# A graph attention layer: q and k as a 257th column of each half of the projection, row scales transposed later

## The reference

```python
h = jnp.maximum(_layernorm(x, axis=-1), 0.0)
q = jnp.einsum('c,bcn->bn', wq, h)
k = jnp.einsum('c,bcn->bn', wk, h)
scores = q[:, None, :] + k[:, :, None]
scores = jnp.where(scores > 0, scores, 0.01 * scores)
att = jax.nn.softmax(scores, axis=-1)
agg = jnp.einsum('bcn,bmn->bcm', h, att)
out = x + jax.nn.relu(jnp.einsum('oc,bcm->bom', wm, agg) + bm[None, :, None])
```

## Time and profile before

| | us |
|---|---|
| median of 3 runs (2089.21 to 2089.91) | 2089.28 |
| the profiled execution, its own time | 2090.47 |
| its span, first to last instruction | 2088.7 |
| PE busy | 2051.5 (98%) |
| DVE busy | 1674.8 (80%) |
| ACT busy | 1221.5 (58%) |
| POOL busy | 379.6 (18%) |
| 3 groups of unit matmuls (L385 to L387), 2048 each | 776 each |
| 3 groups of v tile matmuls (L362 to L364), 1024 each | 389 each |

### The profile page before, as it was taken

How to read it: one execution, slowest core, us unless ns; L and a number is a source line. 1 busy time by engine, 2 the same in 40 slices (tenths; PEclk the granted TensorE clock), 3 DMA queues, 4 the chain that set the end, 5 groups by cost and what they waited for, 6 DMA issues and landing times.

```text
span 2088.7 us, 33534 instructions
## 1 busy us (share of the span) xinstructions
PE 2051.5 (98%) x10448; PEld 950.3 (45%) x10448; DVE 1674.8 (80%) x3661; ACT 1221.5 (58%) x1871; POOL 379.6 (18%) x273
## 2 busy tenths in 40 slices
PE   5899999999999999999999999999999999999999
PEld 2344444444444444444444444444444444444444
DVE  7978878778887788887788877888877888778853
ACT  5556656556655566565566555665655665556634
POOL 1012211112111122111121111221111211112212
PEclk9999999999999999999999999999999999999999
DMA  5244433344324444333433234442334432343332
GB/s 195 64 155 142 148 99 123 138 160 141 133 84 136 151 141 146 104 118 137 161 141 133 84 136 151 141 146 105 117 137 161 141 131 86 136 152 141 106 101 76
DMA packets 126395, 271.46 MB, mean 130 GB/s; under 512 B 22624, under 2 KB 23136, under 8 KB 122208
## 3 DMA queue, kind: packets, MB, share of 16 engines
q1 hardware_dynamic: 123904, 269.01, 37.1%
q10 hardware_dynamic: 2400, 1.58, 0.3%
HBM read 202.91 MB, written 67.63 MB: 130 GB/s over the span
## 4 chain that ended last, share of the span: by engine, by line
PE 95%; DVE 3%; DMA 1%; POOL 0%; issue 0%; ACT 0%; POOLq 0%; SPq 0%; DVEq 0%
PE mix L385 21%; PE mix L387 21%; PE mix L386 21%; PE mix L362 10%; PE mix L363 10%; PE mix L364 10%; PE small L325 2%; DVE den_out L728 1%; PE small L334 1%; DMA xs<-in_x_dram 0%; DVE p_ring L749 0%; DVE p_lo L756 0%; DVE v_lo L761 0%; POOL wm_nat L893 0%; DMA den_row<-den_rows 0%
## 5 line engine op out<-in xcount | busy, mean ns | idle before, releaser
L385 PE MATMUL mix<-p_hi,v_hi 128*128 128x512 f16 x2048 | 776.3, 379 | 5.9 <-DVE p_lo L756 5.4
L386 PE MATMUL mix<-p_lo,v_hi 128*128 128x512 f16 x2048 | 776.2, 379 | 0.0
L387 PE MATMUL mix<-p_hi,v_lo 128*128 128x512 f16 x2048 | 776.2, 379 | 0.0
L911 POOL TENSOR_TENSOR res<-res,y 128x512 f32<-128x512 f32 x256 | 370.5, 1447 | 1688.2 <-ACT y L512 1688.2
L749 DVE SCALAR_TENSOR_TENSOR p_ring<-ab_row,cols,p_ring 128x512 f32<-128x512 f32 x512 | 377.1, 748 | 129.7 <-ACT p_ring L491 129.7
L491 ACT ACTIVATE p_ring<-ab_row,cols 128x512 f32<-128x512 f32 x512 | 349.5, 691 | 192.4 <-DMA ab_row<-ab_rows 132.3
L503 ACT ACTIVATE v_hi<-mix 128x512 f16<-128x512 f32 x256 | 152.7, 597 | 444.1 <-PE mix L364 443.5
L728 DVE SCALAR_TENSOR_TENSOR den_out<-den_row,cols 128x512 f32<-128x512 f32 x512 | 393.4, 806 | 1.0 <-DMA den_row<-den_rows 1.0
L362 PE MATMUL mix<-wmT_hi,h_hi 128*128 128x512 f16 x1024 | 389.1, 380 | 0.0
L364 PE MATMUL mix<-wmT_hi,h_lo 128*128 128x512 f16 x1024 | 388.8, 380 | 0.0
L363 PE MATMUL mix<-wmT_lo,h_hi 128*128 128x512 f16 x1024 | 388.8, 380 | 0.0
(11 more groups left out here) (71 smaller groups left out, 838.9 us busy)
## 6 DMA issues: line engine op xcount, KB each, us to landing
res<-in_x_dram SPq DMA_DIRECT2D x256, 256.0 KB, 3.2
out_dram<-res SPq DMA_DIRECT2D x256, 256.0 KB, 2.1
xs<-in_x_dram SPq DMA_DIRECT2D x124, 512.0 KB, 6.5
den_row<-den_rows SPq DMA_DIRECT2D x32, 1024.0 KB, 4.6
ab_row<-ab_rows SPq DMA_DIRECT2D x64, 512.0 KB, 5.0
res<-in_x_dram SPq DMA_DIRECT2D x4, 512.0 KB, 5.0
wm_nat<-in_adj_dram ACTq DMA_DIRECT2D x1, 1024.0 KB, 12.2
den_rows<-cols SPq DMA_DIRECT2D x32, 8.0 KB, 1.6
```

The costliest lines, as they stand in the source:

```text
L385: pe.matmul(ps[:, :], v_hi[:, b[1], nt, chans], p_hi[:, hf, nt, :], start=(nt == 0), stop=False)
L386: pe.matmul(ps[:, :], v_hi[:, b[1], nt, chans], p_lo[:, hf, nt, :], start=False, stop=False)
L387: mm = pe.matmul(ps[:, :], v_lo[:, b[1], nt, chans], p_hi[:, hf, nt, :], start=False, stop=(nt == NT - 1))
L911: pool.tensor_tensor(res[:, k, :], res[:, k, :], y[:, k % 2, :], ALU.add).then_inc(s_add, 1)
```

## The change

The weights of q and k become a 257th column in each half of the transposed projection weights. A v tile is then 24 matmuls of 257 columns, into a pair of banks, where it was 12 matmuls of 512 into one; with two pairs instead of four banks, tile nt waits for `v_lower` of tile nt-2, and the first two tiles for relu 4 and 5, and for relu 6 and 7. `project_qk` and `select_qk` go away, except that the first batch has a short projection of its own (96 matmuls of two columns). ACT copies the two extra columns out ahead of each `v_upper`. As q and k are complete only with the last tile, `q_head`, `q_tail`, `exponentials` and the trip of the denominators' rows move into the following period; denominators stand behind half 1 as a block. `spread_qmax` moves into unit 0, `transpose_ab` in unit 5 from node tile 2 to node tile 5. ACT's `h_upper`, `h_full` and relu 1 and 2 move behind half 1; relu 6 goes behind step 3 of half 0, relu 7 and `v_upper` 0 behind step 5; `v_lower` 0 goes behind DVE's step 5. At the start POOL scales two of four weight tiles and the q and k weights, DVE scales the other two.

```diff
-        wmT_hi = sb("wmT_hi", [P, CT, O], F16)
-        wmT_lo = sb("wmT_lo", [P, CT, O], F16)
+        wmT_hi = sb("wmT_hi", [P, CT, 2, OH + 1], F16)
+        wmT_lo = sb("wmT_lo", [P, CT, 2, OH + 1], F16)
...
+        pair = [ctx.enter_context(nc.psum_tensor(f"pair{i}", [P, 2, 512], F32)) for i in range(2)]
+        mix = [pair[i // 2][:, i % 2, :] for i in range(MIX)]
...
             def period(b, one, two, three):
+                if one:
+                    write_den_rows(nxt(b))
+                    load_den_rows(nxt(b))
...
-                if two:
-                    write_den_rows(nxt(b, 2))
-                    load_den_rows(nxt(b, 2))
...
+            def project_first_qk():
+
+                pe.wait_ge(s_wqk, 2)
+                pe.wait_ge(s_hlo, CT)
+                for nt in range(NT):
+                    for ct in range(CT):
+                        nodes = slice(nt * P, (nt + 1) * P)
+                        hi, lo = h_hi[:, 0, ct, nodes], h_lo[:, 0, ct, nodes]
+                        w_hi, w_lo = wmT_hi[:, ct, :, OH], wmT_lo[:, ct, :, OH]
+                        pe.matmul(qk_ps[:, nt, :], hi, w_hi, start=(ct == 0), stop=False)
+                        pe.matmul(qk_ps[:, nt, :], hi, w_lo, start=False, stop=False)
+                        mm = pe.matmul(qk_ps[:, nt, :], lo, w_hi, start=False, stop=(ct == CT - 1))
...
             def v_tile(b, nt):
 
-                if nt < MIX and at(b, second):
-                    pe.wait_ge(s_vlo[nt % 2], (nt + MIX) // 2 + 1)
-                elif nt < MIX:
-                    wait(pe, s_y[nt % 2], cnt(b, U // 2, (nt + MIX) // 2 + 1 - U))
+
+                if nt == 0:
+                    pe.wait_ge(s_hlo, cnt(b, CT, CT))
+                if nt < 2 and at(b, second):
+                    pe.wait_ge(s_vlo[nt], NT // 2)
+                elif nt < 2:
+                    for i in range(2):
+                        wait(pe, s_y[i], cnt(b, U // 2, nt + 3 - U))
                 else:
-                    pe.wait_ge(s_vlo[nt % 2], cnt(b, NT // 2, (nt - MIX) // 2 + 1))
-                ps, nodes = mix[nt % MIX], slice(nt * P, (nt + 1) * P)
+                    pe.wait_ge(s_vlo[nt % 2], cnt(b, NT // 2, nt // 2))
+                ps, nodes = pair[nt % 2], slice(nt * P, (nt + 1) * P)
                 for ct in range(CT):
                     if nt == 0 and at(b, first):
-                        pe.wait_ge(s_wl, ct + 1)
+                        pe.wait_ge(s_wl, max(2, ct + 1))
                     hi, lo = h_hi[:, b[1], ct, nodes], h_lo[:, b[1], ct, nodes]
-                    pe.matmul(ps[:, :], hi, wmT_hi[:, ct, :], start=(ct == 0), stop=False)
-                    pe.matmul(ps[:, :], hi, wmT_lo[:, ct, :], start=False, stop=False)
-                    mm = pe.matmul(ps[:, :], lo, wmT_hi[:, ct, :], start=False, stop=(ct == CT - 1))
+                    for half in range(2):
+                        pe.matmul(ps[:, half, 0:OH + 1], hi, wmT_hi[:, ct, half, :],
+                                  start=(ct == 0), stop=False)
+                    for half in range(2):
+                        pe.matmul(ps[:, half, 0:OH + 1], hi, wmT_lo[:, ct, half, :], start=False, stop=False)
+                    for half in range(2):
+                        mm = pe.matmul(ps[:, half, 0:OH + 1], lo, wmT_hi[:, ct, half, :],
+                                       start=False, stop=(ct == CT - 1))
...
                 elif one:
-                    pe.wait_ge(s_vlo[k % 2], cnt(nxt(b), NT // 2, (k + MIX) // 2 + 1))
+                    pe.wait_ge(s_vlo[k // 2], cnt(nxt(b), NT // 2, NT // 2))
                 else:
                     pe.wait_ge(s_y[k % 2], cnt(b, U // 2, (k + MIX) // 2 + 1 - U // 2))
                 ps, chans = mix[k % MIX], slice(ot * P, (ot + 1) * P)
                 for nt in range(NT):
-                    if one and k == MIX + 1 and nt == 2:
+                    if one and k == MIX + 1 and nt == 5:
                         transpose_ab(nxt(b))
+                    if one and (k, nt) == ((1, 2) if at(b, first) else (0, 3)):
+                        spread_qmax(nxt(b))
...
             def v_upper(b, nt):
+
                 act.wait_ge(s_v, cnt(b, NT, nt + 1))
-                act.activation(v_hi[:, b[1], nt, :], mix[nt % MIX][:, :], ACT.Copy,
+                ps = pair[nt % 2]
+                if not at(b, first):
+                    act.activation(qk4[:, nt, :], ps[:, :, OH], ACT.Copy)
+                act.activation(v_hi[:, b[1], nt, :].rearrange("p (h o) -> p h o", h=2), ps[:, :, 0:OH], ACT.Copy,
                                scale=1.0 / H_SCALE).then_inc(s_vhi, 1)
...
                     p_upper(b, NT + nt)
                     if nt < NT - 2:
                         leak(b, NT + nt + 2)
-                    if two and nt in (0, 3, 7):
-                        h_upper(h, (0, 3, 7).index(nt))
-                    if two and nt in (1, 5):
-                        h_full(h, nt // 4)
-                    if nt in (2, 4, 6):
-                        relu(b, nt // 2 - 1)
+                    if one and nt == 1:
+                        exponentials(nxt(b))
+                    if nt == 5:
+                        relu(b, 0)
                 if two:
+                    h_upper(h, 0)
+                    h_full(h, 0)
+                relu(b, 1)
+                if two:
+                    h_upper(h, 1)
+                    h_full(h, 1)
+                relu(b, 2)
+                if two:
+                    h_upper(h, 2)
                     h_upper(h, 3)
                 relu(b, 3)
                 if two:
@@ -543,17 +535,19 @@
                             leak(n, nt + 2)
                         if nt == 0:
                             relu(b, 5)
-                        if nt == 4:
+                        if nt == 3:
                             relu(b, 6)
+                        if nt == 5:
+                            relu(b, 7)
+                            if two:
+                                v_upper(h, 0)
                 else:
                     relu(b, 5)
                     relu(b, 6)
-                relu(b, 7)
+                    relu(b, 7)
                 if two:
-                    for nt in range(NT):
+                    for nt in range(1, NT):
                         v_upper(h, nt)
-                        if nt == 4:
-                            exponentials(h)
...
             def q_head(b):
-                dve.wait_ge(s_qk, cnt(b, 2, 2))
-                for i in range(2):
-                    ins = dve.tensor_copy(qk[:, i, :].rearrange("p (g c) -> p c g", c=2), qk_ps[:, :, :, i])
-                    if i == 0:
-                        q_link(b, 2, ins)
+
+                if at(b, first):
+                    dve.wait_ge(s_qk, 1)
+                    dve.tensor_copy(qk4[:, :, :], qk_ps).then_inc(s_qf, 1)
+                    dve.wait_ge(s_qf, 1)
+                    dve.wait_ge(s_un, 1)
+                else:
+                    dve.wait_ge(s_vhi, cnt(b, NT, NT))
+                q_link(b, 1, dve.tensor_scalar(qk[:, 0, :], qk4[:, :, 0], unscale_q[:, 0:1], None, ALU.mult))
+                dve.tensor_scalar(qk[:, 1, :], qk4[:, :, 1], unscale_q[:, 1:2], None, ALU.mult).then_inc(s_qc, 1)
...
-            def half_0(b):
+                dve.scalar_tensor_tensor(out=v_lo[:, b[1], nt, :].rearrange("p (h o) -> p h o", h=2),
+                                         in0=pair[nt % 2][:, :, 0:OH], scalar=1.0 / H_SCALE,
+                                         in1=v_hi[:, b[1], nt, :].rearrange("p (h o) -> p h o", h=2),
+                                         op0=ALU.mult, op1=ALU.subtract).then_inc(s_vlo[nt % 2], 1)
+
+            def half_0(b, two):
                 weight(b, 0)
                 for nt in range(NT):
                     if nt < NT - 1:
                         weight(b, nt + 1)
                     p_lower(b, nt)
+                    if two and nt == 5:
+                        v_lower(nxt(b), 0)
 
             def early(b, one, two):
                 h = nxt(b, 2)
+                if one:
+                    q_head(nxt(b))
                 weight(b, NT)
                 for nt in range(NT):
                     if nt < NT - 1:
                         weight(b, NT + nt + 1)
-                    if one:
+                    p_lower(b, NT + nt)
+                    if one and nt == 0:
+                        q_tail(nxt(b))
+                if one:
+                    for nt in range(NT):
                         denominator(nxt(b), nt)
-                    p_lower(b, NT + nt)
-                if one:
                     row_scales(nxt(b))
                 if two:
                     h_lower(h, 0)
@@ -792,65 +781,60 @@
             def late(b, one, two, three):
                 h = nxt(b, 2)
                 if one:
-                    half_0(nxt(b))
+                    half_0(nxt(b), two)
                 if two:
-                    q_rows(h)
-                    for nt in range(NT):
```

(65 more changed lines are left out.)

114 lines of the change are left out of this document (31 added, 83 removed).

## The result

The changed kernel takes 2127.27 us (median of 4, 2125.04 to 2128.97) where the kernel before takes 2089.24 (2088.99 to 2089.91) on the same chip: a ratio of 1.0181, 95% interval 1.0163 to 1.0198. It is slower, by 38 us, where 24.5 were forecast.

The account below looks back on a forecast made before the run. PE's own list was taken to set the time. 30 periods by +0.6 (18), start +4.5 and end +2 make 24.5 over the profiled 2090.47: 2115, or 2114 us against the median; range 2060 to 2140.

Parts of the forecast that it names:

- the forecast case: PE waits for relu 7 in each projection, a period of 64.4 us for 63.83; 2105 to 2125 us, chance 63%.
- Sign and mechanism: Slower, since PE stands 1.6 us in v tile 1 of each projection, waiting for ACT's relu 7.
- the late transpose moves relu 7 itself: Transpose at 29.23 us after unit 0, formerly 27.19, delays copy and relu 7; at node tile 2 almost no wait.
- row scales to 25.2: On DVE, half 1 of p and then 16 half denominators leave the row scales ready 25.2 us after unit 0.
- the loss to POOL: Some 0.9 us lost to POOL during the 16 half denominators on DVE, which take 0.67 each.
- PE's list: PE's work per period falls from 63.83 to 62.68 us, with 257-column matmuls at 0.1094 each.
- the small wait: Before unit 0 PE waits for v_lower 6, behind the normaliser on DVE: 0.16 us a period.
- Weight loads under 257 columns: In the projection, loads of 0.10 us hide under matmuls of 0.109; rival that they don't fully, 2142 to 2167, 12%.
- The small waits: Around unit 0: 0.16 us for v_lower 6, and nothing or at most 0.2 for the spread's input.
- Start: First batch and its delays: +4.5 us, between 0 and +19.
- The end: In the last batches, without a projection, half 0 comes 2 us later: +2 us.
- The sum: Whole kernel: 18 us from 30 periods, 4.5 at the start, 2 at the end, together 24.5 us slower.

## Why the prediction was right, and where not

The kernel got slower, as forecast. 2127 lies in the range of 2060 to 2140 and 2 us above the 2105 to 2125 that the forecast case was given.

- **Sign and mechanism: right.** PE stands before the 25th v matmul with ACT's y as releaser, 1.56 us in the period read above (1.6 forecast), with the copy at 29.70 (29.56), the leak at 35.58 (35.54), relu 7 from 45.06 to 45.88 (45.0 to 45.8). Moving relu 7 alone takes the loss away.
- **Why relu 7 is late: wrong step.** "... the late transpose moves relu 7 itself; with the transpose left at node tile 2 the wait would be near nothing." It was not: 2126.75. The failed step is "row scales to 25.2", where 27.4 was measured. The half rows cost 0.673 as forecast, but the loss to POOL is 3.0 us, not the 0.9 of the earlier trace rows and its neighbours: as a block behind half 1, denominators meet three of POOL's adds (at 557.54, 560.40 and 564.27), inside half 1 they met one a period (93 of 512 half rows are long in the changed kernel, 30 before). With h_lower 0 and 1 behind the row scales DVE was busy until 29.70, just when the late transpose would have held it. The dates agreed by luck, because two causes fell on the same one. Where the loss is taken away, the sentence is true: with POOL's adds narrow and the transpose at node tile 2 the wait is 3.5 us in all, 2081.25. The Trainium skill (GPSIMD Engine Reference, "Specifications") lists GpSimd's memory interfaces as shared with VectorE, with contention for DVE instructions that have two SBUF inputs; a denominator has two (both rows of `den_row`), and the trace agrees: 1.75 us where it begins while an add runs, 0.74 otherwise.
- **PE's list: mis-sized.** 62.84 was forecast with the small wait (62.68 and 0.16); the period from the transpose at 571.57 to the next, 64.89, is 63.33 without the 1.56. The matmul of 257 columns costs 0.1117 and not 0.1094: 192 by 0.0023 are 0.44 a period. In the changed kernel the 24 of tile 0 end under the wait for relu 7, so 168 count, 0.39 a period: 11.6 of the 13 us from 2114 to 2127. The reasoning took `project_qk` as the nearest row and its surplus of 1.3 ns as given; there the weight loads were of 32 columns and four groups shared one array. The spread costs 0.22, not 0.11. So the gain on PE's list was 0.50 a period where 0.99 was hoped for.
- **Weight loads under 257 columns: right.** They hide. The rule of the Trainium skill (TensorE: Matmul & The Clock Gate, "What overlaps and what doesn't"), by which they could not, would have given about 0.21 a pair; 0.1117 was measured.
- **The small waits: right.** From the last pair at 541.88 to unit 0 at 542.20 are 0.32, 0.10 more than a pair's 0.22; 0.16 was forecast. The spread costs 0.11 more than a transpose without a wait; its weight load waits for DVE's `qmax_p` 30 times, so this is most likely that wait, which was put at 0 to 0.2.
- **Start: near in sum, wrong in its terms.** Forecast +4.5, measured +3.2 by the third unit 0. The 96 small pairs of the first batch cost 0.027 each, 2.6 us, where 9.6 was put down:

```profile
24.97 0.17 PE L318 MATMUL small<-wmT_lo,h_hi 128*128 128x2 f16 x1
25.00 0.17 PE L319 MATMUL small<-wmT_hi,h_lo 128*128 128x2 f16 x1
25.03 0.17 PE L317 MATMUL small<-wmT_hi,h_hi 128*128 128x2 f16 x1
```

  The first `copy_ab` is sooner than before (67.48 for 68.77), not later. What fills the place are waits that the forecast hadn't: PE waits for `v_lower` three times in the second batch's projection, 8.8 us between 61 and 79 (two pairs of banks, and each tile waits for the tile two before it), and 3.19 us for relu 7 at 134.10, in a period of 66.73. One more term was missing: in the longest of these waits, 5.79 us before 78.25, the granted clock fell to 0.5 (1.2 GHz), from 74.8 to 81.6, and the 16 matmuls behind the wait took 3.40 us, some 1.6 more than at 0.1117. The end is right: +2.2 for the forecast +2.
- **The sum.** 3.2 at the start, 29 by 1.08, 31.3, and 2.2 at the end are 36.7; forecast were 4.5, 18 and 2, together 24.5. So the excess lies in the steady period, 64.9 for 64.4: 0.39 is the pitch, 0.12 is relu 7, behind which PE goes on 46.02 after unit 0 and not 45.9, and the small wait gives 0.06 back.

Open is what the last 3 ns above the columns are in a 257-column matmul, and why the surplus is less at 512.

## What to carry to other kernels

Ask of each bank not when its unit is done but where its evacuation stands in the other engine's list: doubling the banks that a tile needs moved a deadline up by two tiles, and one line moved in ACT's list was worth 42 us. When a step is released by two chains that end within 0.2 us of each other, removing one shows nothing (the transpose), and the right date doesn't prove the cause. A matmul's price at a new width should be bounded by the surplus of like matmuls (same load, same banks): 2.3 ns over 5040 matmuls is 12 us. And a wait on PE can cost more than its own length: look at the granted clock behind it.

## What the runs showed of the hardware that I had not expected

- Matmuls with a 128-column weight load each: 512 moving columns 0.2159, 257 columns 0.1117 in two banks by turns and 0.1102 in one bank at a time; two columns 0.027 (start of the changed kernel).
- A DVE instruction with two SBUF inputs of 512 floats takes 1.75 us when it begins while a POOL add of 512 runs, and 0.74 otherwise. In the changed kernel that holds for all 93 and all 419; the long ones end 0.55 us after the add.
- A turn of DVE's loop, with a body of two periods, costs 2.3 to 2.6 us, seen as "issue".
- The row's trip takes 6.5 to 6.6 us where a store and loads start 2.8 us behind the copy, and 5.9 to 6.0 where they start 3.9 or more behind; that they are the cause is likely, not tried.
- Around waits of 2.0 to 3.5 us for relu 7 PE's granted clock went to 0.5 for 3.4 us in six of 29 periods (POOL's adds narrow), at 1.6 us each; around the 1.1 to 1.8 us of the changed kernel in none.
